# Graph and expert kernel: places of four steps in one register word, a third buffer for a slot's rows, state units and adjacency pieces alternating in the queue

## What is computed

```python
msg = x[src]
summed = jax.ops.segment_sum(msg, dst, num_segments=N_NODES)
aggr = summed / jnp.maximum(cnt, 1.0)[:, None]
return aggr @ W_l + b_l + x @ W_r                      # first network, two such layers, 128 wide
...
h = x @ W_in + b_in                                    # second network, 256 wide
for l in range(L):                                     # three layers
    agg = jax.ops.segment_sum(h[src], dst, num_segments=N) / deg
    logits = jnp.concatenate([h, agg], axis=-1) @ router_W[l] + router_b[l]
    vals, idx = jax.lax.top_k(logits, TOPK)            # 2 of 8 experts for each node
    gates = jax.nn.softmax(vals, axis=-1)
    weak = jax.nn.relu(jnp.einsum('nh,ehf->nef', agg, weak_W[l]) + weak_b[l])
    sh = jax.nn.relu(jnp.einsum('nh,ehf->nef', agg, strong_W1[l]) + strong_b1[l])
    strong = jnp.einsum('nef,efh->neh', sh, strong_W2[l]) + strong_b2[l]
    moe = jnp.einsum('ne,neh->nh', gate_dense, experts)
    h = h + conf * moe
return h @ W_out + b_out
```

## Time and profile before

| what | value |
|---|---|
| median of 3 runs | 2573.72 us (2569.99 to 2582.82) |
| the profiled execution's own time | 2555.54 us |
| its span, first to last instruction | 2553.7 us |
| PE matmul busy | 2043.9 us, 80% of the span |
| DVE, POOL, ACT busy | 907.4, 667.3, 578.7 us |
| chain that ended last | PE 63%, DMA 15%, DVE 13%, issue 5% |
| build loop, aggregations of the second network, slots | about 123 to 500 us; 880 to 1040, 1354 to 1620, 1929 to 2196 us; 1040 to 1330, 1620 to 1906, 2196 to 2485 us |

### The profile page before, as it was taken

One profiled execution on the slowest core, in us unless ns is written; L12 is line 12 of the kernel. 1 busy time (PEld: TensorE's weight loads), 2 busy tenths in 40 slices (PEclk: granted clock), 3 DMA queues, 4 the chain that ended last, 5 costly groups with the idle time before them and its releaser, 6 DMA issues.

```text
span 2553.7 us, 36575 instructions
## 1 busy us (share of the span) xinstructions
PE 2043.9 (80%) x12522; PEld 1588.1 (62%) x12523; DVE 907.4 (36%) x2327; ACT 578.7 (23%) x1160; POOL 667.3 (26%) x611
## 2 busy tenths in 40 slices
PE   2656666509999899888878999888878999888875
PEld 1345555406767677776656777776756777776664
DVE  5566666442234322533332101333332101333323
ACT  0045555540001000222221000232221100222221
POOL 4133443300000013443330111343330112343330
PEclk9855555559999899999998999899998999899996
DMA  6920000197466755343345432243335432243333
GB/s 175 347 77 0 0 0 0 39 390 263 141 184 226 231 190 190 81 74 59 59 79 212 149 121 75 60 80 59 59 73 210 157 120 77 58 75 63 61 51 103
DMA packets 187286, 298.04 MB, mean 117 GB/s; under 512 B 47952, under 2 KB 153094, under 8 KB 187043
## 3 DMA queue, kind: packets, MB, share of 16 engines
q1 hardware_dynamic: 148786, 237.95, 27.8%
q0 software_dynamic: 38384, 58.53, 12.9%
HBM read 179.30 MB, written 117.13 MB: 116 GB/s over the span
## 4 chain that ended last, share of the span: by engine, by line
PE 63%; DMA 15%; DVE 13%; issue 5%; ACT 2%; SPq 1%; DVEq 0%; POOL 0%; ACTq 0%; POOLq 0%
PE psum L1382 20%; PE psum L1498 13%; DMA arena<-xs_d 12%; PE psum L1296 7%; PE psum L1279 6%; DVE arena L729 4%; PE psum L1461 3%; PE psum L1476 2%; DVE arena L1056 2%; DVE arena L1054 2%; PE psum L1250 2%; DMA adj_d<-arena 1%; PE psum L1301 1%; PE psum L1487 1%; PE psum L1275 1%
## 5 line engine op out<-in xcount | busy, mean ns | idle before, releaser
L1382 PE MATMUL psum<-arena 128*128 128x320 bf16 x3750 | 533.1, 306 | 36.4 <-DMA arena<-adj_d 24.4
L1382 PEld LDWEIGHTS psum<-arena 128*128 128x128 bf16 x3750 | 373.9, 100 | 190.7 <-issue 25.2
L646 POOL DMA_INDIRECT h_rows<-arena,idx x192 | 304.0, 1583 | 558.5 <-DVE arena L1056 515.0
L1487 PE MATMUL psum<-arena 128*128 128x256 f32 x1536 | 361.1, 389 | 3.4 <-ACT arena L1208 3.3
L1498 PE MATMUL psum<-arena 128*128 x1536 | 350.3, 381 | 2.6 <-ACT arena L1211 2.2
L1487 PEld LDWEIGHTS psum<-arena 128*128 128x128 f32 x1536 | 281.3, 193 | 67.9 <-ACT arena L1211 19.0
L1498 PEld LDWEIGHTS psum<-arena 128*128 128x128 f32 x1536 | 285.6, 191 | 40.4 <-issue 5.1
L1211 ACT ACTIVATE arena<-psum,b1c 128x256 f32<-128x256 f32 x384 | 181.8, 474 | 490.5 <-PE psum L1487 490.3
L618 POOL DMA_INDIRECT xs_d<-arena,pos x150 | 145.1, 967 | 549.3 <-DVEq L876 507.3
L1296 PE MATMUL psum<-arena 128*128 128x320 bf16 x1500 | 224.9, 302 | 73.7 <-DMA arena<-adj_d 73.7
L729 DVE TENSOR_TENSOR arena<-arena 125x1600 bf16<-125x1600 bf16 x200 | 229.4, 1190 | 135.3 <-PE psum L1279 133.9
(11 more groups left out here) (250 smaller groups left out, 1681.0 us busy)
## 6 DMA issues: line engine op xcount, KB each, us to landing
arena<-adj_d SPq DMA_DIRECT2D x125, 800.0 KB, 4.5
xs_d<-zrow SPq DMA_DIRECT2D x8, 3432.0 KB, 26.7
arena<-xs_d SPq DMA_DIRECT2D x96, 264.0 KB, 3.4
adj_d<-arena SPq DMA_DIRECT2D x25, 800.0 KB, 7.4
arena<-h_rows SPq DMA_DIRECT2D x22, 640.0 KB, 8.7
h_rows<-zrow SPq DMA_DIRECT2D x1, 8192.0 KB, 38.3
arena<-x_d SPq DMA_DIRECT2D x20, 320.0 KB, 3.6
arena<-in_L_gnn_strong_W SPq DMA_DIRECT2D x24, 256.0 KB, 6.7
```

The lines of the kernel that those rows point to most:

```text
L646: pool.indirect_dma_start(h_rows, bass.IndirectOffsetOnAxis(ap=idx[:, j % 2, h:h + 1], axis=0), ybuf[:, j % 2, h], None, compute_op=ALU.ad ...
L1382: mm = pe.matmul(psum[:, q, 0:HN], hs[:, k * SK + s, part, f * P:(f + 1) * P], half(ring[:, k, s], h), start=(k == 0 and s == 0 and part = ...
L1487: mm = pe.matmul(psum[:, 5 + f % 2, 0:M], w1s[:, j % 2, f // 2, kt, f % 2 * P:(f % 2 + 1) * P], xsT[:, j % 2, kt], start=(kt == 0), stop=( ...
```

## The change

There are three parts.

1. In the table a place is now a whole number from 0 to 8, and four steps are packed into one 32-bit word, four bits each. PE loads 16 words once in a pass in place of 32 twice. For each step its sequencer takes the four bits out: an AND for the first of a word, a shift and an AND for the second and third, a shift alone for the fourth, and a multiplication by the new distance of windows in PSUM, `WP` = 103 columns. With that distance no window crosses a bank, so `PAD` goes, and ACT's copy at L1143 reads eight windows of 100 columns in place of two runs of 400. On DVE two instructions of 1600 elements become three of 400.
2. `xsl` has three buffers, and the rows of slot J are asked for when slot J-3 has left its buffer.
3. Behind the slots, unit 3 is followed by piece 0, unit 4, piece 1, unit 5, piece 2, unit 6, piece 3, unit 7, piece 4.

```diff
-GA = 4 * WC
-PAD = 512 - GA
+WP = WC + 3
@@ build
-        w_rel = carve([T], I32, 1)
+        w_rel = carve([T // 4], I32, 1)
-        xsl = carve([2, 2, XW], F32)
+        xsl = carve([3, 2, XW], F32)
-        b_xin = [sem(f"slot_rows_in_{k}") for k in range(2)]
+        b_xin = [sem(f"slot_rows_in_{k}") for k in range(3)]
@@ sync: slots_in
-                    if j > 1:
-                        sp.wait_ge(b_yr, 2 * (J - 1))
-                    sp.dma_start(xsl[:, j % 2], xs_d[bass.ds(at_row[j % LOAD], M)].rearrange("(h p) c -> p h c", p=P)).then_inc(b_xin[j % 2], 16)
+                    if j > 2:
+                        sp.wait_ge(b_yr, 2 * (J - 2))
+                    sp.dma_start(xsl[:, J % 3], xs_d[bass.ds(at_row[j % LOAD], M)].rearrange("(h p) c -> p h c", p=P)).then_inc(b_xin[J % 3], 16)
@@ sync: behind the slots
-                    if u == 3 and p < 4:
-                        expert_pieces(p + 1, 0)
+                    if u >= 3 and p < 4:
+                        expert_pieces(p + 1, 0, (u - 3,))
@@ vector: the table
-            link(v.tensor_scalar(step_no[0:1, 0:T], wf[:, :], 5.0, float(PAD), ALU.is_ge, ALU.mult))
-            v.scalar_tensor_tensor(w_rel[:, :], wf[:, :], float(WC), step_no[0:1, 0:T], ALU.mult, ALU.add).then_inc(s_tab, 1)
+            four = wf[:, :].rearrange("o (s g) -> o s g", g=4)
+            packed = step_no[0:1, 0:T // 4]
+            link(v.scalar_tensor_tensor(packed, four[:, :, 3], 16.0, four[:, :, 2], ALU.mult, ALU.add))
+            link(v.scalar_tensor_tensor(packed, packed, 16.0, four[:, :, 1], ALU.mult, ALU.add))
+            v.scalar_tensor_tensor(w_rel[:, :], packed, 16.0, four[:, :, 0], ALU.mult, ALU.add).then_inc(s_tab, 1)
@@ scalar: supersteps
-                    act.copy(adj[:, bass.ds(off[u] + WC, G * WC)].rearrange("p (b n) -> p b n", b=2), banks[:, :, WC:WC + GA]).then_inc(s_wide, 1)
+                    act.copy(adj[:, bass.ds(off[u] + WC, G * WC)].rearrange("p (w n) -> p w n", w=G),
+                             banks[:, WP:WP + G * WP].rearrange("p (w n) -> p w n", w=G)[:, :, 0:WC]).then_inc(s_wide, 1)
@@ tensor: supersteps
-                    if q % 2 == 0:
-                        n = 2 * k * G
-                        _, rel = nc.values_load_multi_w_load_instructions(
-                            w_rel[0:1, bass.ds(i * (NOH // 2 * n) + q // 2 * n, n)], engines=(EPE,), min_val=0, max_val=G * WC + PAD,
-                            skip_runtime_bounds_check_because="a window's offset in its superstep")
+                    if q == 0:
+                        _, words = nc.values_load_multi_w_load_instructions(
+                            w_rel[0:1, bass.ds(i * (2 * RS), 2 * RS)], engines=(EPE,), min_val=0, max_val=0x8888,
+                            skip_runtime_bounds_check_because="four windows' places in a superstep, four bits each")
@@
-                            mm = pe.matmul(bank[:, bass.ds(rel[(q % 2 * k + g) * G + z], WC)], oh1[:, q, n, :, z % 2], oh2[:, q, n, :, z % 2],
+                            word = words[2 * u + z // 4]
+                            place = word >> 12 if z % 4 == 3 else (word >> 4 * (z % 4)) & 15 if z % 4 else word & 15
+                            place = nc.s_assert_within(place * WP, 0, G * WP, skip_runtime_bounds_check_because="a window's place in its superstep")
+                            mm = pe.matmul(bank[:, bass.ds(place, WC)], oh1[:, q, n, :, z % 2], oh2[:, q, n, :, z % 2],
```

More of the change, by code:

```diff
@@ L459, in _, with expert_pieces @@
                     states(p, b)
-            def expert_pieces(p, b):
+            def expert_pieces(p, b, ks=range(NK)):
                 i = blk(p, b)
-                for k in range(NK):
+                for k in ks:
                     if i == 0:
@@ L1038, in slots @@
                         weights(j + 1)
-                    v.wait_ge(b_xin[j % 2], 16 * (J // 2 + 1))
+                    v.wait_ge(b_xin[J % 3], 16 * (J // 3 + 1))
                     if J > 1:
                         v.wait_ge(b_sc[j % 2], 32 * (J // 2))
-                    step(v.tensor_tensor(idf[:, j % 2], xsl[:, j % 2, :, H + 1], valid[:, j], ALU.mult))
+                    step(v.tensor_tensor(idf[:, j % 2], xsl[:, J % 3, :, H + 1], valid[:, j], ALU.mult))
                     step(v.tensor_tensor(idx[:, j % 2], idf[:, j % 2], lost[:, j], ALU.add))
@@ L1055, in slots @@
                         v.wait_ge(b_yt, 2 * J + h + 1)
-                        v.tensor_scalar(ybuf[:, j % 2, h], ybuf[:, j % 2, h], xsl[:, j % 2, h, H:H + 1], None, ALU.mult).then_inc(b_yr, 1)
+                        v.tensor_scalar(ybuf[:, j % 2, h], ybuf[:, j % 2, h], xsl[:, J % 3, h, H:H + 1], None, ALU.mult).then_inc(b_yr, 1)
             def rest(p, u):
@@ L1135, in supersteps @@
                 for u in range(RS):
-                    banks = psum[:, u % 4 * 2:u % 4 * 2 + 2]
+                    banks = psum[:, u % 4 * 2:u % 4 * 2 + 2].rearrange("p b n -> p (b n)")
                     act.wait_ge(s_step, i * RS + u + 1)
@@ L1140, in supersteps @@
                         act.wait_ge(s_first, i * RS + u - 6)
-                    act.copy(first_w[:, u % 8], banks[:, 0, 0:WC]).then_inc(s_stage, 1)
+                    act.copy(first_w[:, u % 8], banks[:, 0:WC]).then_inc(s_stage, 1)
                     act.wait_ge(s_wide, i * RS + u + 1)
-                    act.copy(adj[:, bass.ds(off[u] + WC, G * WC)].rearrange("p (b n) -> p b n", b=2), banks[:, :, WC:WC + GA]).then_inc(s_wide, 1)
+                    act.copy(adj[:, bass.ds(off[u] + WC, G * WC)].rearrange("p (w n) -> p w n", w=G),
+                             banks[:, WP:WP + G * WP].rearrange("p (w n) -> p w n", w=G)[:, :, 0:WC]).then_inc(s_wide, 1)
             supersteps(0, head=True)
@@ L1470, in slot_turn @@
                 J = slot(p, j)
-                pe.wait_ge(b_xin[j % 2], 16 * (J // 2 + 1))
+                pe.wait_ge(b_xin[J % 3], 16 * (J // 3 + 1))
                 if J:
@@ L1475, in slot_turn @@
                     for h in range(2):
-                        mm = pe.transpose(psum[:, 4, f * M + h * P:f * M + (h + 1) * P], xsl[:, j % 2, h, f * P:(f + 1) * P], ident[:, :])
+                        mm = pe.transpose(psum[:, 4, f * M + h * P:f * M + (h + 1) * P], xsl[:, J % 3, h, f * P:(f + 1) * P], ident[:, :])
                 mm.then_inc(b_turn, 1)
```

## The result

The kernel before took 2571.85 us (median of 4 runs, 2564.01 to 2582.82) and the changed one 2613.6 us (4 runs, 2609.4 to 2614.59): a ratio of 1.0156, 95% interval 1.0116 to 1.0196. The change makes the kernel 42 us slower. I had said 2591 us, 17 us slower.

The account below looks back on a forecast made before the run. PE's sequencer was taken to bound the build loop, late rows the slots, and a late split the stretch behind them. Terms 114 - 82 - 15 = +17 us gave 2572.5 us profiled, 2591 us median; 8-in-10 range 2560 to 2618.

Parts of the forecast that it names:

- 2000 register operations: Build loop, PE's sequencer: each added ALU operation costs 0.092 us from start to start, +184 us in all.
- 1600 fused operations: Build loop, PE's sequencer: these also multiply now, 12 ns more each, +20 us in all.
- loads of places: Build loop: 25 loads of 16 words replace 50 of 32, with their address operations, -89 us.
- table on DVE: Before the build loop: two DVE table instructions become three of a quarter of the length, -1 us.
- third buffer: Slots: the wait for rows goes (-106 us), a late Relu gives back +24 us, net -82 us.
- queue order: Behind the slots: PE's rest of 6.64 us after piece 0 and a similar one go, net -15 us.
- the break-even of 0.083 us: Build loop: the price of one register operation at which the whole change neither gains nor loses.
- One result more is about 10 ns: Build loop: what one more computed result adds to a fused operation's duration, read from operations of 37, 46 and 68 ns.
- the rival of 8.2 us: Slots: POOL's scatter bounds a slot at 8.2 us, kernel +41 us, 2615 us; chance 0.12.
- A rest before piece 1 of over 2 us: Behind the slots: PE resting this long before piece 1 would show the queue part wrong.
- The rival of hidden register operations: Build loop: each operation costs at most its own 32 ns, kernel -123 us, 2451 us; chance 0.15.
- that of dependent ones at 0.12 us: Build loop: dependent register operations wait for each other, 0.12 us each, kernel +73 us, 2647 us; chance 0.08.

Follow-up runs that it names:

- buffers_alone: The kernel before with only the third buffer for a slot's rows: 2462.91 us, ratio 0.9696 to the kernel before.
- queue_alone: The kernel before with only the new order of units and pieces behind the slots: 2523.88 us, ratio 0.9928 to the kernel before.
- whole_again: The whole change measured once more beside the kernel before in the same call: 2578.77 us, ratio 1.0137.
- extra_op: The whole change with one more AND, which changes nothing, in each step of the build loop: 2756.47 us, ratio 1.0848 to the kernel before.
- the waits by part: PE waits for each Relu part where first used: added to parts 2 and 3, 2387.53 us; added to the kernel before, 2537.28 us.

## Why the prediction was right, and where it was off

The side was right, and the mechanisms were those forecast: register work paid in full, rows that come in time with the Relu late in their place, no rest behind piece 0. The size was half of it, +17 us where +42 and +36 were measured. The terms that were too small are those of part 1. The terms:

| term | predicted | measured | from |
|---|---|---|---|
| 2000 register operations | +184 | +194 | 97 ns from start to start, not 92 |
| 1600 fused operations | +20 | +30 | 112 ns to the weight load after 93, not 12 more |
| loads of places | -89 | -88 | the rest of the build loop's +135.8 |
| table on DVE | -1 | -0.2 | three instructions of 0.85 us after 1.8 and 1.0 |
| third buffer | -82 | -79 | buffers_alone |
| queue order | -15 | -18 | queue_alone |
| sum | +17 | +38 (medians of the three parts) | whole_again: +36 |

**What the register operations cost.** This step was sound: each is paid in full, and the break-even of 0.083 us that the prediction names was passed. I took the gap of 0.06 us from five mixed instructions, and it is 0.061. But in the changed kernel an ALU operation mostly lasts 36 ns and not the 32 of the earlier trace rows: with the gap 5 ns more, 10 us. A pass takes 20.4 us, not 19.3. The Trainium skill's issue floor ("Runtime: NRT & Kernel Launch", section "Instruction fetch mechanics"), an estimated 17 ns, is missed by a factor of almost six on this engine: the trace, with 97 ns, does not agree with it as a price.

**The fused operations** are the other half of the miss in part 1. "One result more is about 10 ns" held for three of four: 46 to 55 ns. The fourth has the shift in it as well and takes 83 to 98 ns, mostly 93; most often it costs 46 ns more than before, nearly half of the ALU operation that it replaces. I had asked what a step adds and not what the fourth step's operation holds.

**The third buffer.** The wait for the rows went in all 88 slots, and the period is 7.98 us as forecast. But that the term came so near is partly luck. The output starts 0.91 us behind the turn, and not the 0.76 of the earlier trace rows. From start to start, as a mean over the 93 slots that follow another one in a layer, the way from the hidden layer to the next turn fell from 4.91 to 3.59 us, 123 us in all; from turn to output it grew from 0.51 to 0.91 and from output to hidden layer from 3.48 to 3.55, 44 us together. The sum had -106, the rests that the profile lists, and +24. Each was too small by 17 to 20 us, and the two errors cancel. POOL's scatter was no bound: the rival of 8.2 us is out.

**The queue.** Right, and a little better: 10.1 and 9.6 us in the two layers, where 15 us stood for both. The second rest was shorter, as I had put it (5.34 us), and gave nearly as much. "A rest before piece 1 of over 2 us" didn't come (0.49 us in one execution, none in others).

The rival of hidden register operations (chance 0.15) is out by *extra_op*, and that of dependent ones at 0.12 us too.

**The rest of the miss is small.** The terms measured alone give +38, the first comparison +42 and the later one +36, each within the other's interval or at its edge; these differences are not explained. The profiled execution of before, from which I took 2555.5 us, had lost 7 to 9 us net up to the end of the build loop, as told above. That moved no term but would have spoiled a comparison of the two spans, which differ by 53.7 us.

What stays open: why the start is shorter with the third buffer, and why the first execution of the changed kernel lost 18 us in the aggregations of p = 2. Its trace shows PE resting up to 8.86 us there for ACT's L1173, and ACT for something that the trace puts down to "another core or an unknown queue", while POOL scatters rows. In the aggregations of layer 1 the same execution has rests of up to 1.54 us put to "issue" that *whole_again* has not; they are part of why only 2.6 us of the queue's gain of 10 show there. I made no experiment on any of this.

## What to carry to other kernels

Packing table entries to save register loads pays only if taking them out is cheaper than loading them: here a loaded word costs 0.064 us and each shift or AND 0.097 us from start to start, so even two entries to a word lose. Look for the sequencer's time behind matmuls that never fill their engine. A change with a good half and a bad half looks like a small loss: this one hid 99 us of gain, and one wait moved afterwards brought some 55 more. And try again after each fix what was worth nothing before it: the waits by part gave nothing with two buffers and 0.57 us a slot with three.

## What I had not expected of the hardware

**The matmuls of one stretch get faster at different places.** Ahead of the build loop both kernels run the same matmuls of 400 columns. Their timelines are alike up to 63 us. Then the kernel before has

```profile
64.21 2.93 PE L1250 MATMUL psum<-arena 100*125 100x400 bf16 x8
...
95.90 1.57 PE L1250 MATMUL psum<-arena 100*125 100x400 bf16 x8
```

and the changed kernel

```profile
63.84 1.57 PE L1253 MATMUL psum<-arena 100*125 100x400 bf16 x8
```

Eight matmuls take 2.93 us and then 1.57; the first execution stayed at the slower pace until about 95 us, the second until 63 us, after the same work. The last matmul of the stretch ends 15 us later for it, nearly as much as part 3 brings. The granted clock reads 1.00 over the whole stretch in both profiles. But the clock record in the two traces has its first entry (a clock of 1.00) only at 94.9 and at 63.3 us, where the pace changes, and ahead of any entry the row reads 1.00 whatever the clock is. I take the change of pace for the clock's rise; it is read from this coincidence and from the durations, no entry of the lower level stands ahead of it. In the other profiles the first entry stands at 61.7 to 63.6 us in the kernels with the third buffer and at 78.3 to 78.6 in those with two, which is the difference in the start told above.

**A short bubble.** In the build loop, now and then an instruction of PE's sequencer starts 0.03 us later behind the one ahead of it than its like do, most often 16 or 17 instructions after the last such one. In a pass of *extra_op* (323 instructions) there are 15 to 18, some 0.5 us; in one of the changed kernel (243) 7 to 9.

**The first loads of places are longer, while DMAs run.** Counted from load to load, the first two passes of the changed kernel take 19.5 and 23.1 us, the others 20.4; before, 22.0 and 15.0 where the others take 14.7. It looks like the first way through the loop's code, but the excess is in the loads. Before, the two loads of the first pass take 5.98 and 6.86 us, not 2.13, and in the second pass of the changed kernel the load takes 3.50 and not 1.10. The DMA that fills `h_rows` with zeros lands at 142 us before and at 143 us after, and between 130 and 140 us the DMAs of the kernel before move 385 GB/s. No load of places that starts later in the loop takes over 2.15 us before or 1.12 us after. No experiment separates the DMAs from the code. They would also explain why the late start of the first profile gave back 4 us in the loop: fewer of its loads fall into that time.
